# Masked attention with gated output: a diagonal in three steps, rotary queries stored in four parts, buffers on 128-byte starts

## What is computed

```python
xn = _layernorm(x)
c_Q = xn @ W_DQ.T;  q_C = heads(c_Q @ W_UQ.T);  q_R = rope(heads(c_Q @ W_QR.T), pos)
c_KV = xn @ W_DKV.T;  k_C = heads(c_KV @ W_UK.T);  k_R = rope(xn @ W_KR.T, pos);  v = heads(c_KV @ W_UV.T)
scores = clip(einsum('bhqd,bhkd->bhqk', [q_C, q_R], [k_C, k_R]), -80, 80)
scores = where(pos[:, None] >= pos[None, :], scores, -inf)
s = merge(softmax(scores / sqrt(192)) @ v) @ W_O.T
g = silu(base(xn) + top-2-of-8 low-rank experts(xn))
out = x + s * g
```

## Time and profile before

| | us |
|---|---|
| median of three runs | 1421.35 (1419.82 to 1422.22) |
| profiled execution | 1420.26 |
| its span on the core | 1418.7 |
| PE busy | 1381.4 (97%) |
| DVE busy | 1146.3 (81%) |
| ACT busy | 782.1 (55%) |
| POOL busy | 125.1 (9%) |

### The profile page before, as it was taken

How to read it: one execution, slowest core, us unless ns; L and a number is a source line. 1 busy time by engine, 2 the same in 40 slices (tenths; PEclk the granted TensorE clock), 3 DMA queues, 4 the chain that set the end, 5 groups by cost and what they waited for, 6 DMA issues and landing times.

```text
span 1418.7 us, 27675 instructions
## 1 busy us (share of the span) xinstructions
PE 1381.4 (97%) x9810; PEld 1147.4 (81%) x9810; DVE 1146.3 (81%) x1339; ACT 782.1 (55%) x861; POOL 125.1 (9%) x175
## 2 busy tenths in 40 slices
PE   7999689999999999999999999999999999999998
PEld 6888568778888888888888889888899688878887
DVE  7666378898898898988889898898788888967664
ACT  4232367666666666666566665666665656533221
POOL 0000111101101101010010100111100011022121
PEclk9999899999999999999999999999999999999999
DMA  8322665645435423333242422444412233166552
GB/s 304 121 88 101 176 190 152 177 131 160 119 94 141 120 95 91 123 84 120 66 119 85 116 99 63 122 151 140 131 56 63 67 109 118 52 199 172 169 158 89
DMA packets 110769, 174.91 MB, mean 123 GB/s; under 512 B 9608, under 2 KB 65160, under 8 KB 108168
## 3 DMA queue, kind: packets, MB, share of 16 engines
q1 hardware_dynamic: 93880, 108.99, 25.1%
q0 software_dynamic: 16016, 63.80, 15.7%
q10 hardware_dynamic: 832, 1.57, 0.5%
HBM read 125.83 MB, written 48.50 MB: 123 GB/s over the span
## 4 chain that ended last, share of the span: by engine, by line
PE 74%; DVE 8%; ACT 3%; DMA 3%; issue 1%; POOL 0%; ACTq 0%; SPq 0%; DVEq 0%; POOLq 0%
PE score_ps L1242 29%; PE out_ps L1264 19%; PE score_ps L1361 3%; PE score_ps L1362 3%; PE score_ps L1363 3%; DVE prob_l L1558 2%; PE out_ps L1283 1%; ACT prob_h L1421 1%; PE out_ps L1284 1%; PE out_ps L1287 1%; PE score_ps L1212 1%; DMA rot_l<-turned 1%; DVE prob L1545 1%; DVE prod L1517 1%; PE score_ps L1213 1%
## 5 line engine op out<-in xcount | busy, mean ns | idle before, releaser
L1421 ACT CAST prob_h<-prob 128x1024 fp32r<-128x1024 f32 (+1 forms) x288 | 289.8, 1006 | 236.1 <-DVE prob L1540 188.7
L1558 DVE TENSOR_TENSOR prob_l<-prob,prob_h 128x1024 fp32r<-128x1024 f32 (+1 forms) x288 | 335.9, 1166 | 39.6 <-ACT prob_h L1421 38.2
L1415 ACT ACTIVATE prob<-score_ps 128x1024 f32<-128x1024 f32 (+1 forms) x288 | 281.8, 979 | 148.8 <-PE score_ps L1242 99.3
L1242 PE MATMUL score_ps<-q_h,key_slot 64*128 64x512 f32 x1792 | 363.7, 391 | 0.0
L1264 PE MATMUL out_ps<-prob_h,value_slot 64*128 64x512 f32 (+1 forms) x1792 | 348.7, 377 | 1.8 <-DMA value_slot<-values 1.0
L1553 DVE TENSOR_TENSOR total<-total,prob 128x1024 f32<-128x1024 f32 (+1 forms) x256 | 294.7, 1151 | 0.0
L1540 DVE TENSOR_SCALAR prob<-prob 128x1024 f32<-128x1024 f32 x224 | 155.1, 692 | 72.0 <-ACT prob L1415 71.7
L1264 PEld LDWEIGHTS out_ps<-prob_h,value_slot 64*128 64x128 f32 x1792 | 178.3, 184 | 38.2 <-DVE prob_l L1558 6.6
L1242 PEld LDWEIGHTS score_ps<-q_h,key_slot 64*128 64x128 f32 x1792 | 178.2, 184 | 30.6 <-issue 5.0
L1242 PE MATMUL score_ps<-q_l,key_slot 64*128 64x512 f32 x896 | 181.1, 390 | 0.0
L1242 PE MATMUL score_ps<-rot_hh,key_slot 64*128 64x512 f32 x896 | 180.9, 389 | 0.0
(11 more groups left out here) (210 smaller groups left out, 2000.5 us busy)
## 6 DMA issues: line engine op xcount, KB each, us to landing
key_slot<-keys SPq DMA_DIRECT2D x144, 256.0 KB, 2.7
value_slot<-values SPq DMA_DIRECT2D x144, 128.0 KB, 2.3
rot_hh<-turned POOLq DMA_DIRECT2D x30, 512.0 KB, 6.2
heads_rows<-head_rows POOLq DMA_DIRECT2D x15, 1024.0 KB, 9.7
turned<-rot_hl POOLq DMA_DIRECT2D x14, 1024.0 KB, 5.2
rows<-heads_rows SPq DMA_DIRECT2D x28, 512.0 KB, 5.8
rot_l<-turned POOLq DMA_DIRECT2D x30, 256.0 KB, 7.7
x_in<-in_x SPq DMA_DIRECT2D x16, 256.0 KB, 2.7
```

What stands on the lines that cost most here:

```text
L1242: mm = pe.matmul(score_ps[:, half, c * 512:(c + 1) * 512], keys_of[ROWS[r], :], moving[par][ROWS[r], half * HW + c * 512:half * HW + (c + ...
L1415: nc.scalar.activation(prob[half][:, 0:width], score_ps[:, half, 0:width], ACT.Exp, scale=QK_SCALE).then_inc(exp_done, 1)
L1421: nc.scalar.copy(prob_h[half][:, 0:width], prob[half][:, 0:width]).then_inc(high_done, 1)
L1558: nc.vector.tensor_tensor(p_l, p, p_h, ALU.subtract).then_inc(split, 1)
```

## The change

Five things change.

1. **Diagonal tiles.** Each diagonal tile's early 64 queries see only its first 64 keys. `late_scores` does the late 64 queries of all 8 heads in five passes of 512 columns, and the early 64 in ten matmuls of 256 columns whose weights are the first 64 keys beside 64 zero columns (`early_keys`, loaded by two new DMAs a unit), so that the two groups of four heads land in the upper and the lower 64 partitions. One such step is 768 columns. A unit's two diagonal steps and `second_scores` (the second token tile against the corner's keys, 1024 columns) replace the four halves before: ACT and DVE do three steps. The mask is 2 x 64 columns; the totals of the early queries are kept apart by head group with a factor of 0 or 1 (`sides`).
2. **Order of values.** `weigh_second` (whole array) stands between the straight and crossed pairs of the first full tile; `weigh_late` for the late tile is last in that pair. It uses the whole array for the late queries and 64-row pairs for the early ones, the lower pair from `value_early` (again two new DMAs a unit). Buffers of `prob` and `score_ps` are picked by `buffer_of`.
3. **Queries by tile.** Queries stand by token tile first, so `turned` has another layout: a gather reads 2048 floats in a row, a store is four DMAs. In prepare, unit 1's stores go from SP to POOL.
4. **Order of reads.** In a corner whose predecessor is a late tile, ACT copies the first result half out after the second cast.
5. **Buffers.** `edge` (96 bytes) is put at the right end, `causal` is halved, `sides` added and used in place of `spread_first`. All large buffers then begin on multiples of 128 bytes.

```diff
+EDGE = 24
+TURNED_PARTS = 4
+def turned_parts(unit, rot_hl):
+    halves = raw(rot_hl).rearrange("p w e (c x) -> p (w e) c x", c=2)
+    for q in range(4):
+        home = unit.rearrange("f w e (h c q x) -> f (w e) h c q x", h=2, c=2, q=2)[:, :, q // 2, :, q % 2, :]
+        yield home, halves[q * HALF:(q + 1) * HALF, :, :, :]
...
+        ctx.enter_context(nc.sbuf_tensor("edge", [P, EDGE], F32, side="right"))
...
+def buffer_of(par, kind, half):
+    return half ^ par ^ 1 if kind == FULL else half ^ par
...
+            def load_early_keys(unit, k, kind):
+                late = kind == LATE
+                if not late:
+                    since(sp, early_scored, unit.n)
+                since(sp, early_keys_in, 16 * (2 * unit.n + late))
+                sp.dma_start(raw(early_keys[:, :, DQ:P]), one_of(keys, k)...[:, :, 0:DQ]).then_inc(early_keys_in, 16)
...
-                    pool.dma_start(turned[bass.ds(n + 2, 1), :, :, :].rearrange("a w p n -> p (a w) n"),
-                                   raw(rot_hl[:, :, :, :]).rearrange("p w e n -> p w (e n)")).then_inc(passed, 16)
+                    for home, source in turned_parts(unit, rot_hl):
+                        pool.dma_start(home, source).then_inc(passed, 16)
...
+                def late_part():
+                    for n, (keys_of, moving) in enumerate(blocks):
+                        mm = pe.matmul(score_ps[:, buffer, 0:512], keys_of, tile_of(moving[par][:, :], c)[:, :, :, DQ:P], ...)
+                def early_part():
+                    pe.wait_ge(early_keys_in, 16 * (2 * unit + c + 1))
+                    for n, (_, moving) in enumerate(blocks):
+                        for half in range(2):
+                            mm = pe.matmul(score_ps[:, buffer, 512:DW], early_keys[:, block_of[n], (1 - half) * DQ:(1 - half) * DQ + P],
+                                           tile_of(moving[par][:, :], c)[:, half, :, 0:DQ], ...)
...
+            def weigh_late(t, n, slot, buffer, c, last):
+                for half in range(2):
+                    for step, (word, weights) in enumerate(passes):
+                        pe.matmul(bank(half)[:, :, DQ:P], value_slot[slot][:, word:word + P],
+                                  heads(weights[buffer][:, half * 256:(half + 1) * 256]), ...)
+                for word, weights in passes:
+                    for half, (rows, values_of) in enumerate(zip(ROWS, (value_slot[slot], value_early))):
+                        mm = pe.matmul(bank(half)[:, :, 0:DQ], values_of[rows, word:word + P],
+                                       heads(weights[buffer][rows, 512:DW]), start=False, ...)
+                mm.then_inc(weighed, 2 if c == 1 else 1)
...
                         for crossed in (False, True):
-                            half_scores(full, half, par, keys_of, crossed)
-                            half_weigh(full, t - 1, half, 1 - slot, prev, crossed)
+                            half_scores(full, half, par, keys_of, buffer, crossed)
+                            if prev == FULL:
+                                half_weigh(full - 2, t - 1, half, 1 - slot, buffer, crossed)
+                            elif not crossed:
+                                weigh_second(t - 2, half, slot, buffer_of(par, CORNER, 1), n if unit.has_second else None)
+                            elif half == 1:
+                                weigh_late(t - 1, n, 1 - slot, buffer, 1, False)
...
+                    since(pe, sums_read, n)
+                    since(pe, out_read, 2 * n)
+                    weigh_late(t, n, slot, buffer_of(par, CORNER, 0), 0, not has_full(unit))
...
-                exponential(0)
-                if prev is not None:
+                exponential(0, DW, 2 * t + 1, 2 * t - 2 if late_before else 2 * t - 1)
+                if prev == FULL:
                     act.wait_ge(weighed, 2 * t - 1)
                     read_out(n - 1, 0)
-                high(0)
-                exponential(1)
-                begin(0)
-                high(1)
+                high(0, DW, 2 * t + 1, 2 * t - 2 if late_before else 2 * t - 1)
+                since(act, summed, unit.added)
+                exponential(1, HW, 2 * t + 2, 2 * t)
+                begin_late()
+                high(1, HW, 2 * t + 2, 2 * t)
+                if late_before:
+                    act.wait_ge(weighed, 2 * t)
+                    read_out(n - 1, 0)
...
-            def clip(t, n, half, kind):
+            def clip_late(buffer, step, signals):
+            def add_late(n, step, par, buffer):
```

515 lines of the change are left out of this document (311 added, 204 removed).

## The result

The changed kernel takes 1441.57 us (median of 4 runs, 1438.74 to 1442.36), the kernel before 1421.64 beside it (median of 4): the ratio is 1.0141, with a 95% interval of 1.0129 to 1.0153. The forecast was 1416.5, 4.9 less than before, with a range up to 1427, so it was wrong, by 25 us and with the wrong sign. The profiled run took 1442.1 (span 1440.6); its span stands against the 1418.7 of before.

A forecast was written before the change was run, and what follows sets the result against it. PE's matmul slots were taken to bound nearly everything, the start treated apart. +0.3 - 2.5 + 5.2 + 2.5 - 9.4 - 1.0 = -4.9 on 1420.26 gave 1415.4, plus 1.1 for the median: 1416.5 us, range 1406 to 1427.

The forecast's parts named there:

- What bounds the kernel: Whole kernel: PE's matmul slots set the end nearly everywhere; PE waits only between 150 and 205 us.
- Rotary queries in four stores: Start: longer gather rows shorten PE's first gather wait, -2.5 us (-1 to -4); first-stage stores cost +0.3 (0 to +1.5).
- They end about with the last y stores: End of first stage: unit 1's stores on POOL finish about with SP's y stores, +0.3 us (0 to +1.5).
- Early keys and values are 4 more loads a unit on SP, each behind a load with the same deadline: nothing: SP's queue in each unit: the extra loads cost nothing, as those loads have 2 us and more to spare.
- Units 1 to 3: Start: sum_up waits for ACT's later copy; unit 2 begins 0.3 later, unit 3 6.5; +5.2 us (+1 to +7).
- The half clock: Behind PE's idle time at sum_up in units 1 and 2: granted clock 0.50 costs another 1.2 us.
- The diagonal's slots and switches: Units' diagonal work: slots -0.70, eight tiling switches +1.52, DVE waits up to -0.75 a unit; +2.5 over 12 units (-4 to +8).
- The DVE stalls: First two full tiles: PE's waits for prob_l go, saving 0.5 us in an even unit, 0.75 in an odd one.
- the walk: Queues followed from a corner's start: second full tile begins at 24.0 to 24.6 us, nothing late.
- Right-hand buffers: Even units and last stage: aligning right-hand buffers to 128 bytes brings even halves to 3.400 us, -9.4, and last stage -1.0.
- The last stage's term: Last stage: one streamed operand in three comes from an aligned right-hand buffer, -1.0 us (0 to -2).
- Rival A: Right-hand buffers: place, not alignment, makes slots long; the -10.4 us goes, giving 1426.9; chance 12%.

The follow-up runs named there:

- a_keys: Changed kernel with SP issuing unit 2's first keys and unit 1's late-tile keys before the early-value loads that wait for weigh_late: 1436.35 us, ratio 1.0104.
- a_lat: Changed kernel; in units 1 and 2 ACT copies the first half out after its second exponential, sum_up runs between the latents' halves: 1430.92 us, ratio 1.0067.
- a_noedge: Changed kernel without the 96 bytes in front of the right-hand buffers: 1449.88 us, ratio 1.0195.
- a_qoff: Changed kernel with the 96 bytes moved behind the right-hand queries, so total0 and rows0 stay aligned and the queries do not: 1451.85 us in one run.
- b_edge: Kernel before with 96 bytes in front of the right-hand buffers, nothing else: 1419.14 us, ratio 0.9983.
- a_swap: Changed kernel with the two homes of prob, prob_h and prob_l exchanged: 1437.03 us in one run.

## Why the prediction was wrong, step by step

**What bounds the kernel** held: PE's slots from unit 4 on, the start by waits. The failure is in the start.

**Rotary queries in four stores** is the step that failed worst. It gave the whole gather the pace of a store of 4 KB runs, 1 MB in 5.2 us, though only two of its four DMAs got longer rows (2 KB to 8 KB), and left the new stores at the old pace, though their runs fell from 4 KB to 1 KB. The end of the first stage cost 6.2 us instead of 0.3, and the first gather, from ACT's issue at 156.97 to PE's start at 169.78, took 12.8 instead of 11.8, where 2.5 less was forecast. Loads of early keys, 128 KB in runs of 256 bytes, are in flight beside it; what they cost it was not run apart. "They end about with the last y stores" looked at issues, where the DMA digits of the stage were at 9 throughout.

**"Early keys and values are 4 more loads a unit on SP, each behind a load with the same deadline: nothing"** is the step that failed in kind. It priced the loads by their deadlines and not by what each waits for before it is issued. In units with full tiles that is right: PE's wait for value_slot in all of them is 0.6 us. In units 0 and 1 the early values wait for weigh_late, and the next unit's keys stand behind. They landed 0.7 and 3.2 us behind the gather, and a_keys took 2.2 us out of PE's waits and 5.2 out of the time, part of it clock. Once issued during a gather they took long: issued at 182.01, landed 8.1 later, where the load issued at 175.74 in a_keys, ahead of the gather, took 2.6. The Trainium skill (DMA: Bandwidth & Descriptors, Queues, rings and completion order) has each DMA engine take turns between its queues packet by packet; 2.6 us becoming 8.1 beside a gather agrees with that, but no run here shows how the turns were shared.

**Units 1 to 3**: right in mechanism for sum_up of unit 2 (7.7 us between units 2 and 3, 6.2 forecast), though with a wait of 3.15 and not 5 to 6, so the near size is partly luck. For unit 1 the step said that the wait hides in unit 2's wait for its gather. It did not, since the gather itself is issued only when the latents behind sum_up are done: 208.94, 18.8 after unit 1's start, where it was 11.5 before. What comes later starts later. a_lat measured the two waits together at 10.6 us, of which the profiles place 10.1 in these two units. (The +5.2 is also a slip of 0.3: 6.5 later less a wait of 1.0 is 5.5.)

**The half clock** is the term that was mis-sized in all of this. The step charged 1.2 us behind a wait. Counted in half microseconds, PE worked 27.8 us at 0.50 between units 0 and 4, in five stretches of 4.7 to 6.1, against 5.7 in two before; at half pace that costs 13.9 against 2.9, so by this count 11 of the 18.9 us, about as much as the waits themselves grew (9.7).

**The diagonal's slots and switches** held in kind and came out larger: a_noedge against before, which have the same right-hand offsets, gives +4.1 in the even units and +2.4 in the odd ones, 6.4 in all where 2.5 was forecast (-4 to +8). Every switch costs 0.33 + 0.34 against 0.23 + 0.23, and PE reaches unit 13's second full tile 24.81 after the corner's start (946.71 - 921.90), where the walk said 24.0 to 24.6. The DVE stalls went. Odd units 5 to 13 are 0.3 longer each and unit 15 is 0.8, 0.1 was forecast; the walk came out short because a slot up to there takes 0.235 to 0.24, where I had taken 0.23.

**Right-hand buffers** was sized nearly right and explained by half. Forecast -9.4 and -1.0; a_noedge against the changed kernel gives -8.5 in the even units and -3.4 in the last stage, and a_qoff ties both to the queries and merged_l. The last stage's term was put too low. Rival A, that 96 bytes make no difference, fell. With it falls what the Trainium skill's 16-byte lines (SBUF — State Buffer, Specifications) would give, by which an offset of 96 is as good as any: a_qoff and the changed kernel differ only in that offset, and in 11.6 us from unit 4 on. But the term was argued as a property of the streamed buffer alone, and b_edge showed that it is not: there it brings 2.1 of 11.9. That the forecast had nearly the right number for the changed kernel is luck, since the change moved the left-hand buffers as well, which no part of it said.

**The range** left out what it did not look at. The rivals were about steady units and about losing less at the start; none had the start lose more, in the 120 us between 145 and 262, where the change touched every queue at once.

## What to carry to other kernels

When a change adds a load to a queue, write down for it and for what stands behind it which semaphore it waits for, not only when its data is wanted; do this for the short stages at the start, where queues are not yet far ahead. When a layout changes, price both sides by the length of the contiguous run, store and gather, and put the sum against the DMA's busy share there. Price a wait on the path with the half clock behind it, which here cost as much as the waits. And where two stretches run the same instructions at different pace, try addresses early: one unused tensor of a few KB brought 0.7% here, where all the reordering cost time.

## What the runs showed of the hardware

- Pairs of 64-row matmuls that stream 512 columns take 3.400 us for 15 pairs in a row or 3.47 to 3.49, by the addresses of what they stream (a multiple of 128, or 96 past it) together with those of the left-hand buffers; unit 12 lasted 99.89 to 99.91 in all eight kernels of the changed order with aligned queries and 101.73 in both without (a_noedge, a_qoff), so it is not noise.
- Stores of the same 3.15 MB ran at 312 GB/s with runs of 4 and 2 KB and at 194 with runs of 1 KB (and another place in HBM) for two thirds of them, on either queue.
- Straight and crossed pairs on the same banks, with nothing between, cost 0.33 us, nearly as much as two switches of tiling.
- Behind PE's waits of 3.15 to 7.55 us in the changed kernel the granted clock was 0.50 (1.2 GHz) for 4.7 to 6.1 us of work, which costs half of that. It is not the same each time: behind the same wait of 3.15 us it was 1.00 in a_swap and a_noedge, and behind the 6.74 us ahead of unit 0 in the kernel before it was 0.50 for 2.8 us.
